# Base rows in the output tensor, attention rows added there by accumulating scatters, and the gate's product taken before the normalisation

## The reference

```python
xn = layernorm(x)
x = x + gnn(xn, edges) + mix(xn)      # edge attention, 8 heads; linear attention
x = x + ffn(layernorm(x))             # mixture of 8 experts, one per row, capacity 977
# ffn(h): logits = h @ gate_w + gate_b;  idx = argmax(softmax(logits))
#         pos = running count of rows with this idx;  kept = pos < 977
#         y = (relu(h @ w1[idx] + b1[idx]) @ w2[idx] + b2[idx]) * prob * kept
```

## Time and profile before

| | us |
|---|---|
| median of 3 runs | 2846.49 (2846.21 to 2849.05) |
| the profiled execution's own time | 2847.4 |
| its span, first to last instruction | 2846.2 |
| PE, DVE, ACT, POOL busy | 2110.9, 2397.0, 1029.1, 2103.6 |

### The profile page before, as it was taken

The page is one execution under the profiler, slowest core; times in us unless marked ns, Lnnn a source line. Parts: engine busy times, 40 slices in busy tenths (PEclk is TensorE's granted clock), DMA queues, the critical chain, the costliest instruction groups (busy, mean ns, idle before and its releaser), DMA issues. The chain is left out here.

```text
span 2846.2 us, 36156 instructions
## 1 busy us (share of the span) xinstructions
PE 2110.9 (74%) x9360; PEld 1696.3 (60%) x9361; DVE 2397.0 (84%) x3259; ACT 1029.1 (36%) x4377; POOL 2103.6 (74%) x2223
## 2 busy tenths in 40 slices
PE   6976777766667777688888776666656637599998
PEld 5764566655556666466666554444444427499997
DVE  6867999988889999999999888899999956366765
ACT  4434666656566666211111111011111106345453
POOL 6767777777777777777777777777777765578785
PEclk9988999999998898889999877778787875699999
DMA  7769777777777777888888877777777749333331
GB/s 239 267 230 322 219 219 218 218 219 217 218 219 218 218 218 213 249 230 255 261 257 255 247 224 211 211 211 211 211 210 211 211 159 293 107 77 89 80 90 15
DMA packets 257952, 586.96 MB, mean 206 GB/s; under 512 B 49583, under 2 KB 135678, under 8 KB 257722
## 3 DMA queue, kind: packets, MB, share of 16 engines
q0 software_dynamic: 150448, 467.11, 58.4%
q1 hardware_dynamic: 98135, 109.52, 11.7%
q10 hardware_dynamic: 9296, 9.44, 1.0%
HBM read 519.06 MB, written 71.84 MB: 208 GB/s over the span
## 5 line engine op out<-in xcount | busy, mean ns | idle before, releaser
L1036 POOL DMA_INDIRECT wide<-kv_d,arena x1099 | 1052.4, 958 | 339.7 <-issue 326.4
L1333 PE MATMUL ps<-wide,arena 128*128 128x264 f32 x2432 | 698.9, 450 | 232.4 <-DVE wide L1435 232.2
L1333 PEld LDWEIGHTS ps<-wide,arena 128*128 128x128 f32 x2432 | 534.1, 225 | 389.1 <-DVE wide L1435 275.6
L1036 POOL DMA_INDIRECT arena<-kv_d,arena x539 | 515.2, 956 | 164.3 <-issue 160.0
L1171 ACT ACTIVATE ps<-wide 128x256 f32 x229 | 88.8, 388 | 1267.3 <-DVE arena L1401 1263.7
L1404 DVE TENSOR_REDUCE arena<-arena 128x64 f32<-128x2048 f32 x229 | 523.9, 2288 | 7.9
L1333 PE MATMUL ps<-arena 128*128 128x264 f32 x1216 | 350.4, 451 | 132.6 <-DVE arena L1435 132.4
L1401 DVE TENSOR_TENSOR arena<-wide,ps 128x2048 f32<-128x2048 f32 x153 | 349.5, 2284 | 88.1 <-DMA wide<-kv_d,arena 88.0
L1333 PEld LDWEIGHTS ps<-arena 128*128 128x128 f32 x1216 | 266.7, 225 | 212.8 <-DVE arena L1435 157.5
L140 PE MATMUL ps<-halves 128*128 128x256 f32 (+2 forms) x2304 | 362.1, 319 | 3.2 <-DVE halves L1696 1.6
L1435 DVE TENSOR_TENSOR wide<-wide,ps 128x2112 f32<-128x2112 f32 x152 | 356.8, 2347 | 0.0
(11 more groups left out here) (338 smaller groups left out, 3096.9 us busy)
## 6 DMA issues: line engine op xcount, KB each, us to landing
wide<-kv_d,arena POOLq DMA_INDIRECT x1099, 3.8
arena<-in_w SPq DMA_DIRECT2D x16, 1024.0 KB, 5.5
kv_d<-wide SPq DMA_DIRECT2D x49, 260.0 KB
arena<-xn_d SPq DMA_DIRECT2D x82, 128.0 KB, 3.5
arena<-kv_d,arena POOLq DMA_INDIRECT x539, 3.8
hb_d<-arena SPq DMA_DIRECT2D x16, 516.0 KB, 6.1
xn_d<-arena SPq DMA_DIRECT2D x7, 896.0 KB
base_d<-arena ACTq DMA_DIRECT2D x49, 128.0 KB, 3.5
```

What stands on the lines that cost most here:

```text
L1036: e.indirect_dma_start(out=kvb[k][:, j, :], out_offset=None, in_=kv_d, in_offset=bass.IndirectOffsetOnAxis(ap=ixb[k][:, j:j + 1], axis=0)) ...
L1333: m = e.matmul(psE[(k + 1) % 3][:, 0:264], ident, kvb[b][:, j, 256:ROW], start=(j == 0), stop=(j == J - 1))
```

## The change

The base row tiles are stored to out directly, and no base_d or at_d exists. The 49 scatters of attention rows go to out with `compute_op=ALU.add` and a bounds check; POOL waits before the first of them for the stores of the base rows. The gate stage loads a group once, from out, and neither adds the halves nor stores the sum.

The order of the gate stage changes too. PE transposes the raw sums as soon as a group is there, and the gate's product is taken on them. This needs weights whose columns have mean zero (gw less its column means, made once by a PE product and a DVE operation), and the logits are then multiplied by the row's inverse root (one more DVE operation per group). ACT's normalisation stays, since the experts' rows need it, but comes three tiles behind the transposes, and POOL's scatters wait for it. `spread2` of the next group moves from the first to the fifth tile of a group.

```diff
-        base_d = dram("base_d", [NP, D])
-        at_d = dram("at_d", [NP, D])
...
         def attention_in(grp):
-            t_x2[grp] = dma(Y, XH[:, tiles_of(grp), 0:256], at_d[grp * 896:grp * 896 + 896, :].rearrange("(t p) d -> p t d", p=128), s_x2[grp])
-
-        def base_in(grp):
-            n_, r0, c0 = (7 if grp < 6 else 6), grp * 896 + 128, place(7 * grp)
-            t_x2[grp] = dma(Y, XH[:, c0:c0 + n_, 256:512], base_d[r0:r0 + 128 * n_, :].rearrange("(t p) d -> p t d", p=128), s_x2[grp])
+            n_, r0, c0 = (7 if grp < 6 else 6), grp * 896, place(7 * grp)
+            t_x2[grp] = dma(Y, XH[:, c0:c0 + n_, 0:256], out[r0:r0 + 128 * n_, :].rearrange("(t p) d -> p t d", p=128), s_x2[grp])
...
             s_we[0].inc(e.dma_start(w1r, kpart(w1[0])), 16)
-            base_in(0)
-            base_in(1)
             e.wait_ge(s_ag.h, 16 * NT)
             attention_in(0)
             attention_in(1)
...
             e.wait_ge(s_in[3].h, 16)
+            for k in range(RING):
+                e.wait_ge(e_bs[k], 16 * (AUX + (k == RING - 1)))
             for c in range(NT):
                 e.wait_ge(e_ao, c + 2)
-                e.indirect_dma_start(out=at_d, out_offset=bass.IndirectOffsetOnAxis(ap=sortedi[:, c, 0:1], axis=0),
-                                     in_=qs[:, c, :], in_offset=None).then_inc(s_ag.h, 16)
+                e.indirect_dma_start(out=out, out_offset=bass.IndirectOffsetOnAxis(ap=sortedi[:, c, 0:1], axis=0), in_=qs[:, c, :],
+                                     in_offset=None, bounds_check=N - 1, oob_is_err=False, compute_op=ALU.add).then_inc(s_ag.h, 16)
...
-                e.dma_start(base_d[bass.ds(val(e, u, 48 * 128), 128), :], xm[k]).then_inc(e_bs[k], 16)
+                    e.dma_start(out[bass.ds(val(e, u, 47 * 128), 128), :], xm[k]).then_inc(e_bs[k], 16)
...
+        tm = sp.inc(product(ps[3][:, 0:8], [(ones, gw[:, k, :]) for k in range(2)]))
+        wait(V, tm)
+        t_gw = v(V.scalar_tensor_tensor(out=gw, in0=ps[3][:, 0:8].unsqueeze(1).to_broadcast([128, 2, 8]), scalar=-1.0 / D, in1=gw,
+                                        op0=ALU.mult, op1=ALU.add))
+
         def turn_h(u):
-            wait(T, t_h[u], t_hT.get(u - 3))
+            wait(T, t_x2[u // 7], t_hT.get(u - 3))
...
         def logits(grp):
...
-            t_ld[grp] = v(V.tensor_tensor(e3(L)[:, grp * 7:grp * 7 + 7, :], e3(gate_ps[grp % 2][:, 0:56]),
-                                          gbias.unsqueeze(1).to_broadcast([128, 7, 8]), ALU.add))
+            seq(V.tensor_tensor(l, e3(gate_ps[grp % 2][:, 0:56]), rss[grp % 2].unsqueeze(2).to_broadcast([128, 7, 8]), ALU.mult))
+            t_ld[grp] = v(V.tensor_tensor(l, l, gbias.unsqueeze(1).to_broadcast([128, 7, 8]), ALU.add))
...
-            wait(G, t_sl, t_hz)
+            wait(G, t_sl, t_hz, t_h[c1 - 1])
...
-            t_sum[grp] = v(V.tensor_tensor(part[:, :, 0:256], part[:, :, 0:256], part[:, :, 256:512], ALU.add))
-            wait(V, t_sum[grp])
...
-        for s_ in range(NT + 3):
+        t_sd_, t_sq_ = {0: spread2(0)}, {}
+        for s_ in range(NT + 4):
             grp, i = divmod(s_, 7)
-            if i == 0 and grp < 7:
-                t_o = out_group(grp)
-                if grp + 1 < 7:
-                    t_sd_ = spread2(grp + 1)
-                wait(S, t_nm[grp])
+            if i == 4 and 1 <= grp < 6:
+                t_sd_[grp + 1] = spread2(grp + 1)
             if s_ < NT:
-                center_h(s_)
+                turn_h(s_)
             if 0 <= s_ - 1 < NT:
-                turn_h(s_ - 1)
-            if 0 <= s_ - 2 < NT:
-                u = s_ - 2
+                u = s_ - 1
                 gate(u)
...
+            if i == 1 and grp < 7:
+                t_sq_[grp] = root2(grp, t_sd_[grp])
+            if i == 2 and grp < 7:
+                t_nm = scale2(grp, t_sq_[grp])
+                if grp == 0:
+                    t_sd_[1] = spread2(1)
+            if 0 <= s_ - 3 < NT:
+                if (s_ - 3) % 7 == 0:
+                    wait(S, t_nm)
+                center_h(s_ - 3)
             advance()
```

More of the change, by code:

```diff
@@ L873, in gps_layer_kernel @@
         e_so, e_si, e_sa, e_sd, e_se, e_sl, e_sg = [esem(n) for n in ("so", "si", "sa", "sd", "se", "sl", "sg")]
-        l_fin, l_tp, l_at, l_wo, l_ao, l_sc = [esem(n) for n in ("lfin", "ltp", "lat", "lwo", "lao", "lsc")]
+        l_fin, l_tp, l_at, l_wo, l_ao, l_df, l_sc = [esem(n) for n in ("lfin", "ltp", "lat", "lwo", "lao", "ldf", "lsc")]
         XH = R12[:, 0:NT * XW].rearrange("p (t w) -> p t w", w=XW)
@@ L888, in attention_in @@
         def attention_in(grp):
-            t_x2[grp] = dma(Y, XH[:, tiles_of(grp), 0:256], at_d[grp * 896:grp * 896 + 896, :].rearrange("(t p) d -> p t d", p=128), s_x2[grp])
-        def base_in(grp):
-            n_, r0, c0 = (7 if grp < 6 else 6), grp * 896 + 128, place(7 * grp)
-            t_x2[grp] = dma(Y, XH[:, c0:c0 + n_, 256:512], base_d[r0:r0 + 128 * n_, :].rearrange("(t p) d -> p t d", p=128), s_x2[grp])
+            n_, r0, c0 = (7 if grp < 6 else 6), grp * 896, place(7 * grp)
+            t_x2[grp] = dma(Y, XH[:, c0:c0 + n_, 0:256], out[r0:r0 + 128 * n_, :].rearrange("(t p) d -> p t d", p=128), s_x2[grp])
             if grp == 6:
-                t_x2[grp] = dma(Y, XH[:, place(48), 256:512], base_d[0:128, :], s_x2[grp])
+                dma(Y, XH[0:N - 48 * 128, place(48), 0:256], out[48 * 128:N, :], s_x2[grp])
+                t_x2[grp] = dma(Y, XH[N - 48 * 128:128, place(48), 0:256], x[0:NP - N, :], s_x2[grp])
         loop = ExitStack()
@@ L1068, in late_tile @@
                 e.nop().then_inc(e_dm, 1)
-                e.wait_ge(l_ao, ld)
+                e.wait_ge(l_df, ld)
                 e.nop().then_inc(e_dm, 1)
-                e.indirect_dma_start(out=at_d, out_offset=bass.IndirectOffsetOnAxis(ap=permc, axis=0), in_=o_row, in_offset=None
-                                     ).then_inc(l_sc, 16)
+                e.indirect_dma_start(out=out, out_offset=bass.IndirectOffsetOnAxis(ap=permc, axis=0), in_=o_row, in_offset=None,
+                                     bounds_check=N - 1, oob_is_err=False, compute_op=ALU.add).then_inc(l_sc, 16)
             (cnt_,) = regs(e, "g_", ["cnt"], [1])
@@ L1114, in tile_end, with base_out @@
                     e.reg_add(o_at, o_at, QI)
-            def base_out(k):
+            def base_out(k, tail=False):
                 e.reg_add(bc, bc, 1)
@@ L1121, in base_out @@
                 e.wait_ge(e_bc, bd)
-                e.dma_start(base_d[bass.ds(val(e, u, 48 * 128), 128), :], xm[k]).then_inc(e_bs[k], 16)
-                e.reg_add(u, u, 128)
+                if tail:
+                    e.dma_start(out[48 * 128:N, :], xm[k][0:N - 48 * 128, :]).then_inc(e_bs[k], 16)
+                else:
+                    e.dma_start(out[bass.ds(val(e, u, 47 * 128), 128), :], xm[k]).then_inc(e_bs[k], 16)
+                    e.reg_add(u, u, 128)
             def take_raw():
@@ L1179, in _, with body @@
             indices(0)
-            def body(k, mix=False, join=None, aux=False, i=0):
+            def body(k, mix=False, join=None, aux=False, i=0, tail=False):
                 record()
@@ L1195, in body @@
                 if aux:
-                    base_out((k - 2) % RING)
+                    base_out((k - 2) % RING, tail)
             def first_out():
                 for k in range(RING):
-                    body(k, aux=k > 0)
+                    body(k, aux=k > 0, tail=k == 1)
             def last_out():
@@ L1506, in late_tile @@
                 divide(mo[0], l_fin)
+                e.wait_ge(e_ao, NT + 1)
+                e.nop().then_inc(e_dm, 1)
+                e.wait_ge(l_ao, ld)
+                e.tensor_tensor(o_row, o_row, qsf[:, bass.ds(val(e, tl, NT - 1) * QI, 256)], ALU.subtract).then_inc(l_df, 1)
                 e.wait_ge(l_sc, sg_)
@@ L1521, in gps_layer_kernel @@
             attention_in(grp)
-            base_in(grp)
         hT = [r3(IDX[:, 512 + 256 * i:768 + 256 * i], 128) for i in range(3)]
@@ L1532, in gps_layer_kernel @@
         void = R3[:, 4400:4401]
-        t_sum = {}
         wait(V, t_fin)
@@ L1548, in gps_layer_kernel @@
         t_rt = [None]
-        s_o, s_sc = sem("s_o"), sem("s_sc")
+        s_sc = sem("s_sc")
         def seq(ins):
@@ L1554, in gps_layer_kernel @@
         gate_ps = [ps[7], ps[2]]
+        tm = sp.inc(product(ps[3][:, 0:8], [(ones, gw[:, k, :]) for k in range(2)]))
+        wait(V, tm)
+        t_gw = v(V.scalar_tensor_tensor(out=gw, in0=ps[3][:, 0:8].unsqueeze(1).to_broadcast([128, 2, 8]), scalar=-1.0 / D, in1=gw,
+                                        op0=ALU.mult, op1=ALU.add))
         def turn_h(u):
             pt = ps[4 + u % 3]
-            wait(T, t_h[u], t_hT.get(u - 3))
+            wait(T, t_x2[u // 7], t_hT.get(u - 3))
             for k in range(2):
-                m = T.transpose(pt[:, k * 128:(k + 1) * 128], XH[:, place(u), 256 + k * 128:256 + (k + 1) * 128], ident)
```

(20 more changed lines are left out.)

1 line of the change is left out of this document (removed).

## The result

| | median us | range, runs | ratio to before, 95% |
|---|---|---|---|
| before | 2846.21 | 2842.81 to 2849.05, 5 | |
| changed | 2860.35 | 2858.48 to 2862.46, 5 | 1.0052 (1.0038 to 1.0066) |

The change makes the kernel 14.1 us slower, 0.5%, clear of noise. Forecast were 2864.0 and a range of 2856 to 2877.

The account below looks back on a forecast made before the run. POOL was taken as the bound, through its attention scatters and last hb_d scatter. Terms +28.2 + 1.4 − 1.2 − 10.95 = +17.5 on 2847.4 gave 2864.9, the runs' median 0.9 lower: 2864.0, range 2856 to 2877.

Parts of the forecast that it names:

- What bounds: POOL never rests in the loop; its 49 attention scatters, 64 us, and its last hb_d scatter set the end.
- The price of an adding scatter: Attention scatters at the loop's end: 1.57 us each, pitch 1.87 instead of 1.283, 48 times, +28.2 us.
- Landing of the last one: Last attention scatter before the barrier: lands in 3.8 us against 2.4, and T0 (DVE's first instruction behind the barrier) follows; +1.4.
- Fewer DMAs: Gate stage: seven base loads and seven stores to out go, so POOL's hb_d scatters are less disturbed; −1.2 us.
- The gate stage: Logits come earlier, so POOL starts on group 2 at T0+43.0 instead of T0+53.95; −10.95 us.
- PE's wait for DVE: Gate stage, L1605: PE's 7.1 us wait is taken as gone, since the statistics moved behind the route.
- Cheap adding scatters: Rival at the attention scatters: adding costs POOL no more than plain; sum −10.8, 2835.7 us; chance 5%.
- Dear scatters: Rival: attention scatters run at the experts' median or worse, +33 to +50 us, 2869 to 2886; chance 13%.
- A gate stage that gives little back: Rival: PE still waits for DVE or ACT's order raises the pitch; some 4 us won, 2872; chance 10%.
- a rising clock: Rival: TensorE's clock rises above 0.50 in the gate stage, POOL starts group 2 earlier, down to 2855; chance 4%.

Follow-up runs that it names:

- e1: The changed kernel with its 49 attention scatters plain, without the add, so base rows are lost; 2832.04 us, ratio 0.9955.
- e4: e2 with every group routed by itself, seven batches instead of five; 2833.43 us, ratio 0.9959.
- e6: The changed kernel with seven batches of one group in the gate stage; 2852.14 us, ratio 1.0023.
- e9: e4 with the stores of the sums to out as 49 of 128 KB in place of 7 of 896 KB; 2831.77 us, ratio 0.9961.
- e12: e4 with each of DVE's seven adds cut into seven pieces; 2832.69 us, ratio 0.9954.
- e7: The kernel before, with POOL itself waiting at the block's end for the scatters' landing, then a memset of one element; 2851.28 us, single time.
- e8: The kernel before, with SP not waiting in the block for the landing and loading groups 0 and 1 behind the barrier; 2847.36 us, single time.
- e10: e4 without the stores of the sums to out, so base and attention rows are missing from its output; 2834.17 us in one run.
- e3: The changed kernel's storage (accumulating scatters, no add or stores of sums) with the old order of the gate stage; 2861.03 us, ratio 1.0057.
- e2: The kernel before with the new order of the gate stage alone, on the old storage with plain scatters; 2836.77 us, ratio 0.9973.
- e5: The changed kernel with adding attention scatters of 64 rows instead of 128, half the attention rows left out; 2844.4 us, single time.

## Why the prediction was right, and where a step failed

*What bounds.* Right. The 49 attention scatters lie on the path from the first to the last, and the gate stage is worth what it moves POOL's last scatter to hb_d: in e1 to e4, e6 and e9 to e12 the stretch behind the stage stays at 394.6 to 396.0 us, whatever the stage does.

*The price of an adding scatter.* Right, +27.65 for +28.2. The median is 1.541, the least of the experts' scatters in the earlier trace rows, and 47 of the 49 took under 1.63 us. That DVE's loop work would hardly disturb them was right as well.

*"Landing of the last one … +1.4 … SP, and through the barrier every engine, is queued behind it. T0 follows the landing by the same 7.2 us."* This step failed. The landing did grow by 1.3 us (2.43 to 3.75), but it was never on the path. The barrier is held by POOL's drain: on the old storage it ends 8.4 us behind POOL's last work whether or not a scatter is outstanding (e7), and comes as late when SP doesn't wait for the landing at all (e8). In the changed kernel it ends 6.8 us behind. So the piece is the last scatter, 0.57 us longer, and a drain 1.6 us nearer, −1.03 instead of +1.4, while the gap from landing to T0 fell from 7.24 to 4.89. Why the drain is nearer stays open. This step makes 2.4 of the 5.1 us by which the sum missed; nearly all the rest, 2.5 us, are the loop's start and the experts' tail, which the change doesn't touch.

*"Fewer DMAs … their removal shows as less disturbance of POOL … −1.2."* The size was right (35 scatters in 45.0 us where they took 46.0), since it was the whole excess of the old scatters, whatever made it; the cause was wrong. Without any store the scatters stay slow (e10); with the add in pieces they are not (e12). It was the add's leaving. The same add also slowed POOL's split of the weights: L1706 took 7.37 us, the changed kernel's L1704 5.52, and with the add in pieces it takes 5.75 (e12).

*The gate stage.* POOL started on group 2 at T0+43.2, predicted 43.0, and ended at T0+88.2, predicted 87.9; on group 0 it started at T0+16.0, as worked out, and group 3's logits came at T0+37.25, predicted 37.1. So the steps fit and not only their sum. PE's pitch and its granted clock of 0.50 (1.2 GHz) stayed. I had taken PE's wait for DVE as gone; 3.2 us of it are left, but before group 3's logits none (in before 3.0), and 2.5 in the last batch, which POOL reaches later anyway. I had put this down to moving the statistics. e3 shows that the new storage removes it as well, in the old order.

*The rivals.* Cheap adding scatters: excluded by e1 against the changed kernel. That includes what I had drawn from the Trainium skill's "DMA: Bandwidth & Descriptors", section "Anatomy of one DMA — SWDGE (gpsimd) path": the added time lies on POOL, 0.57 us for each DMA, and only 1.3 us once in the landing. Dear scatters: only two took over 1.7 us, 1.787 at the most. A gate stage that gives little back, and a rising clock: neither came.

*Is the order worth having?* Yes, on the old storage: e2 is 0.27% faster than before, and with batches of one e4, e9 and e12 are 0.4 to 0.5% faster, the best of this study and not to be told from each other.

## What to carry to other kernels

Before an HBM round trip is replaced by an accumulating DMA, count the DMAs on the issuing engine and not the bytes: here half of the 12.9 MB that no longer move are the stores of the sums, which had cost nothing (e10), while 49 adds cost 28 us between the first scatter and the last, because POOL was the engine on the path. A change with two parts should be timed in its parts: the order alone made the kernel 0.27% faster (e2), the storage alone 0.57% slower (e3). And a batch that waits for two groups idles the engine that already has one.

## What the runs showed of the hardware that was not expected

POOL's drain at the end of a block takes about 8.4 us behind POOL's last work, in before, e5 (64 rows, adding) and e7, and 6.8 us behind adding scatters of 128 rows (2368.48 to 2375.29 in the changed kernel). Why it is shorter there stays open. In before the record of DVE's drain is 0.017 us long and SP's 0.128. The changed kernel's, which ends at 2375.29:

```profile
L1517 POOLq DRAIN  x1: 28291/28291/28291, 2347.0 to 2347.0; - x1
```

DVE's add with both operands in SBUF holds up an indirect DMA on POOL: beside a 2.02 us add a scatter takes up to 2.76 us in before and 2.55 in e10 instead of 0.98, beside pieces of it 1.10 at the most (e12). It is not the length of DVE's instruction alone. In the loop of before DVE's instructions with one operand in PSUM, or with one operand only, are longer, and attention scatters that begin during them take 0.96 to 0.99:

```profile
2292.80 2.28 DVE L1401 TENSOR_TENSOR arena<-wide,ps 128x2048 f32<-128x2048 f32 x1
2293.25 0.96 POOL L1083 DMA_INDIRECT at_d<-wide,arena  x1 [0.30 <-issue]
```

The Trainium skill, "SBUF — State Buffer", section "SBUF: two separate sides", says that a DVE operation with two SBUF inputs and a GpSimd operation that reads SBUF lock each other out of a shared port pair, whichever starts first, for the whole instruction. The traces agree in one direction, if issuing an indirect DMA, which takes its row numbers from SBUF, counts as such an operation of POOL. In the other they do not show it: in e10 an add that began 0.02 us behind a scatter took 2.03 us, the scatter 0.98.
